# Seven instead of six seven-product pairs in the first row group, one instead of two new ones in the second

## The reference

```python
F = 5120                                       # x is (1024, 10240), W1 (256, 5120), fp32
x1, x2 = (x[:, :F], x[:, F:])
h1 = leaky_relu(layer_norm(x1 @ W1.T))         # layer_norm has no eps, no scale; leak 0.05
h2 = leaky_relu(layer_norm(x2 @ W1.T))
h1 = leaky_relu(layer_norm(h1 @ W2.T))         # W2 (64, 256)
h2 = leaky_relu(layer_norm(h2 @ W2.T))
h = jnp.concatenate([h1, h2], axis=-1)
h = leaky_relu(layer_norm(h @ W3.T))           # W3 (8, 128)
return h @ W4.T                                # W4 (1, 8)
```

## Time and profile before

| | us |
|---|---|
| median of 3 runs | 232.88 (232.81 to 232.94) |
| the profiled execution, its own time | 233.68 |
| its span in the profile | 231.9 |
| PE busy in the span | 224.6 (97%), 999 matmuls |
| DVE busy | 191.4 (83%) |
| ACT busy | 151.7 (65%) |
| POOL busy | 28.8 (12%) |
| DMA | 51.93 MB, mean 224 GB/s |

### The profile page before, as it was taken

How to read it: one execution, slowest core, us unless ns; L and a number is a source line. 1 busy time by engine, 2 the same in 40 slices (tenths; PEclk the granted TensorE clock), 3 DMA queues, 4 the chain that set the end, 5 groups by cost and what they waited for, 6 DMA issues and landing times.

```text
span 231.9 us, 2894 instructions
## 1 busy us (share of the span) xinstructions
PE 224.6 (97%) x999; PEld 179.3 (77%) x999; DVE 191.4 (83%) x245; ACT 151.7 (65%) x240; POOL 28.8 (12%) x41
## 2 busy tenths in 40 slices
PE   6999999999999999999999999999999999999992
PEld 2678786888887888888868888888888878888772
DVE  2689999978959999997669699999989699979324
ACT  3797989859588598963678453665546484824630
POOL 0000020020100200000012224427001400000014
PEclk9999999999999999999999999999999999999995
DMA  5999999999879999446839958668677414150000
GB/s 178 370 378 373 409 341 294 347 272 343 290 214 371 340 276 296 171 161 230 300 54 231 291 164 275 228 212 245 215 251 251 148 69 128 56 181 1 3 0 1
DMA packets 17950, 51.93 MB, mean 224 GB/s; under 512 B 2772, under 2 KB 3156, under 8 KB 17936
## 3 DMA queue, kind: packets, MB, share of 16 engines
q1 hardware_dynamic: 16064, 48.86, 60.5%
q0 software_dynamic: 1872, 2.89, 8.0%
HBM read 50.95 MB, written 0.01 MB: 220 GB/s over the span
## 4 chain that ended last, share of the span: by engine, by line
PE 82%; DMA 5%; DVE 4%; ACT 4%; issue 1%; POOL 1%; SPq 1%; POOLq 0%; DVEq 0%
PE acc L1004 79%; DMA xe_raw<-x 5%; PE acc L1126 2%; DVE xe_lo L703 2%; ACT xe_hi L588 2%; ACT unused L542 1%; DVE x_sum L758 1%; PE acc L1139 1%; ACT xt_hi L588 1%; DVE x_sum L768 1%; ACT we_hi L548 0%; POOL inv L485 0%; ACT stage L548 0%; PE acc L1147 0%; PE acc L1155 0%
## 5 line engine op out<-in xcount | busy, mean ns | idle before, releaser
L1004 PE MATMUL acc<-xe_lo,we_hi 128*128 128x512 f32 x176 | 68.8, 391 | 0.3 <-DVE xe_lo L703 0.2
L1004 PE MATMUL acc<-xe_hi,we_lo 128*128 128x512 f32 x176 | 68.5, 389 | 0.0
L703 DVE TENSOR_TENSOR xe_lo<-xe_raw,xe_hi 128x1024 fp32r<-128x1024 f32 (+1 forms) x48 | 55.6, 1177 | 15.2 <-ACT xe_hi L588 15.1
L588 ACT CAST xe_hi<-xe_raw 128x1024 fp32r<-128x1024 f32 (+1 forms) x48 | 47.9, 1009 | 30.7 <-PE acc L1004 22.1
L1004 PE MATMUL acc<-xe_hi,we_hi 128*128 128x512 f32 x176 | 48.3, 391 | 0.0
L1004 PEld LDWEIGHTS acc<-xe_lo,we_hi 128*128 128x128 f32 x176 | 33.0, 188 | 8.4 <-issue 1.7
L1004 PEld LDWEIGHTS acc<-xe_hi,we_hi 128*128 128x128 f32 x176 | 32.9, 188 | 7.4 <-issue 0.7
L1004 PEld LDWEIGHTS acc<-xe_hi,we_lo 128*128 128x128 f32 x176 | 33.1, 188 | 6.7
L588 ACT CAST xt_hi<-x_sum 128x2048 fp32r<-128x2048 f32 x14 | 26.7, 1910 | 12.8 <-DVE x_sum L774 12.8
L703 DVE TENSOR_TENSOR xt_lo<-x_sum,xt_hi 128x2048 fp32r<-128x2048 f32 x14 | 32.0, 2289 | 1.9 <-ACT xt_hi L588 1.9
L1004 PE MATMUL acc<-xt_lo,ws_hi 128*128 128x512 f32 x64 | 25.0, 391 | 0.1
(11 more groups left out here) (107 smaller groups left out, 274.4 us busy)
## 6 DMA issues: line engine op xcount, KB each, us to landing
xe_raw<-x SPq DMA_DIRECT2D x51, 512.0 KB, 5.5
xs_raw<-x SPq DMA_DIRECT2D x14, 768.0 KB, 5.8
stage<-w SPq DMA_DIRECT2D x21, 256.0 KB, 5.8
x_sum<-x SPq DMA_DIRECT2D x10, 256.0 KB, 3.4
x_sum<-x SPq DMA_DIRECT2D x4, 512.0 KB, 4.5
x_sum<-x POOLq DMA_DIRECT2D x4, 512.0 KB, 8.0
xe_raw<-x SPq DMA_DIRECT2D x2, 256.0 KB, 4.2
stage<-w SPq DMA_DIRECT2D x2, 128.0 KB, 3.3
```

The lines of the kernel that those rows point to most:

```text
L588: act.copy(hi_of(u, part), raw_of(u, part)).then_inc(hi_ready[part.buffer], 1)
L703: dve.tensor_tensor(lo_of(u, part), raw_of(u, part), hi_of(u, part).bitcast(F32), ALU.subtract)\
L1004: return pe.matmul(acc[:, bank, :], w, x, start=first, stop=True, skip_group_check=True)
```

## The change

The first group has seven instead of six S units and thirteen instead of fourteen E units; the S units with transfers that add are S2 to S6 (five) instead of S2 to S5 (four). In the second group the count of S units stays eight, but only one of them (pair 7) is new, instead of two (pairs 6 and 7). The first group's order goes from EHE SEE SEE SEE SE SE SEEL to EHE SEE SE SE SE SE SE SEEL. `centre_w23` follows S4 (unit 12), the same unit as before, when it was S3.

```diff
-SEVEN = 6
-MIXED = 2
+SEVEN = 7
+MIXED = 1
 BOTH = SEVEN + MIXED
...
-ORDER = ("EHE" + "SEE" * 3 + "SE" * 2 + "SEEL", "FE" + "SE" * 8 + "D")
+ORDER = ("EHESEE" + "SE" * 5 + "SEEL", "FE" + "SE" * 8 + "D")
...
-                if es[0].n == W23_UNIT + 3:
+                if es[0].n == W23_UNIT + 4:
                     centre_w23()
```

## The result

| | kernel before | changed kernel |
|---|---|---|
| first comparison, median | 232.91 us (232.81 to 233.38, 4 runs) | 235.08 us (233.85 to 236.16, 4 runs) |
| ratio, 95% interval | | 1.008 [1.0048, 1.0111] |
| second comparison, later, median | 233.26 us (35 runs) | 233.65 us (232.19 to 237.36, 12 runs) |
| ratio, 95% interval | | 1.0027 [0.9996, 1.0058] |

The changed kernel is slower by 0.8% in the first comparison. In the second it reads 0.3% slower, but the interval takes in 1, so no difference is shown there. I had forecast 232.04. The medians are over all runs; the ratios leave out runs more than 1.5% above the fastest of their kernel, one of the changed kernel's twelve (237.36) among them.

A forecast was written before the change was run, and what follows sets the result against it. PE was taken as the bound from 39 us on, feeders only needing to be early. Savings 0.68 + 0.16 = 0.84 us, so 232.88 - 0.84 = 232.04 us; range 231.9 to 233.8.

The forecast's parts named there:

- PE's saving of 0.68 us: Group 0, units 7 to 11: an S unit replaces an E unit, 3 matmuls less at 0.2267 us each.
- 0.16 us of the SEE: Two SEE of units 6 to 11 disappear with their late second E units; their 0.16 us counted as won.
- Group 1, "worth nothing": One new S unit less relieves DVE, ACT and SP, but PE's own 90.31 us hides it; no gain.
- DVE's ledger: Table for S2 to S6 of third-sum starts, weights' lo ends and PE's need times; leads of 1.25 to 2.31 us.
- The chain load, add, third sum: After lo of T: load, 4.77 us to the add's issue, its landing, then third sum two S units later.
- 56.93 + L: Landing time of S4's adding transfer, L being its latency; with 9.8, DVE waits 0.96 us and PE loses nothing.
- rival 2: Adding transfers eat the gain: S4's latency over 10.1, S5's third sum too late; 232.88, no change; chance 0.23.
- S4 alone late: Only S4's adding transfer is late; PE waits its latency minus 10.1 through S5's third sum.
- Rival 3: Slower: adding-transfer loop bounds at S5's third sum, costing twice the latency over 10.1; 233.85 at 11; chance 0.15.
- What would show it wrong: PE idle before S5's weights' lo near 82.4 after DVE waits for x_sum, or E-unit casts releasing PE.
- its figure of 358 GB/s: HBM-to-core rate making the SE period 11.0 us, longer than PE's; set aside for a 421 GB/s window.
- The Trainium skill's rule on GpSimd's descriptors: GpSimd-issued transfers wait during certain DVE two-port modes, so adds slowest where DVE is gapless; given no time.

The follow-up runs named there:

- small_later: Changed kernel with the W2/W3 centring moved to DVE's idle spot inside unit 20 and the small W2, W3, W4 loads eight units later; median 233.67 us, ratio 1.001.
- before_one_new: Kernel before with W1's sums of pair 6 left out in the second group, so one new S unit instead of two (probe only); median 232.80 us, ratio 0.9995.

## Why the prediction was wrong

- *PE's saving of 0.68 us, and 0.16 us of the SEE:* right; S1 to S4 took 30.60 us, and the stretch without adds agrees.
- *Group 1, "worth nothing":* wrong by 0.30 us. I read PE's unbroken 90.31 us as proof that nothing waits there. The chain merges matmuls over short gaps; a late weight load costs its time without a break in the row. The starts of the units would have shown it, as I had used them in group 0: in the kernel before, that period is 10.50 us instead of 10.20.
- *DVE's ledger:* DVE's pace was right to 0.01 us. Its latest times for PE were 0.22 us too late, since it took the matmul (0.68 us) where the weight load (0.46 us) waits: the latest third sum of S5 is 78.06, not 78.28, and that of S4 67.86, where 68.22 was measured.
- *The chain load, add, third sum:* this is the step that failed: "56.93 + L", "I take 9.8" and "No loss, but nearly". L for S4 was 10.0, nearly as taken. The load leg was the mis-sized term: I took 4.77 us (4.80 with the issue) from a place where no add was under way, and it was 6.0 for S4 and 6.6 for S5. Of the 1.49 us by which S4's third sum came later than forecast (68.22, not 66.73), 1.24 are this leg and 0.2 are L. With the leg and the weight load as measured, the L at which PE begins to wait at S5 is not 10.1 but about 8.6, which the 9.8 that I took is over. S3's add took 9.9 where I took 8.5; that cost DVE 0.77 us, but PE nothing. The rows for the load leg were there: 42.16 and 57.85 are loads issued while no add moves, and after the change the loads of two blocks for S4, S5 and S6 are issued into the previous unit's add. I had counted that adds come closer together and priced it in the mean load of the DMA engines (9.7 of 10.2 us), not in the latency of the one request that waits.
- *Rivals 2 and 3* named the place (S5's third sum) and the releaser (lo of the S weights). What both profiles of the changed kernel show is the case that rival 2 called "S4 alone late", with L at 10.0 and 9.9, at which its formula gives no wait. Rival 3's rule, that the L's of S3 and S5 add up, is not what held PE there; small_later's profile comes nearest to it, with 9.4 for S3 and 11.4 for S5. The range to 233.8 stopped at L = 11. Latencies seen at 7.5 to 9.8 us with a threshold that is in truth at 8.6 should have had a much larger chance and a longer tail.
- *The size:* the profile closes at -0.84 - 0.30 + 1.75 = +0.61 us in the stretch. The median of the first comparison was 2.17 us over the kernel before, so some 1.6 us of it are in no profile of the changed kernel. small_later's run of 235.19 shows how such a loss can come about; that the changed kernel's slower runs are like it is an inference.
- *What would show it wrong* came as listed: DVE waiting for x_sum, then PE's wait before lo of S5.
- *The Trainium skill's rules:* its figure of 358 GB/s (page "SBUF — State Buffer", section "A bandwidth-pool intuition that's wrong (but worth ruling out)") would have given the right sign. I had set it aside by one window at 421 GB/s. Over 45 to 85 us the changed kernel moved 282, 349, 285 and 315 GB/s in the four windows of 10 us at a DMA share of 0.95 to 1.07. The kernel before moved 278, 328, 289 and 299 at 0.92 to 1.03 in the same windows and PE lost nothing to DMA there, and the changed kernel's first three periods took 10.20 us each, not the 11.0 of that estimate. So the mean rate does not tell the two apart, and the page's cause is not shown. A peak window was still the wrong row for a queue that must be served in time.
- *The Trainium skill's rule on GpSimd's descriptors* (page "SBUF — State Buffer", section "SBUF: two separate sides"): it is about DVE in two-port modes, and I read it as one about DVE being busy. No run here shows which mode DVE's operations were in, and none was made to test the rule. Adds of 6.0 to 11.4 us occurred with DVE doing the same kinds of work, so how busy DVE was does not explain them. What does, beyond the small loads perhaps, stays open.

## What to carry to other kernels

When a change brings two transfers of one dependent chain closer together, price the chain with each leg's latency while the other is under way; the mean load of the DMA engines does not show it. Where the latency of a transfer scatters by more than the lead in hand, keep a spacing rather than a maximum of offloading: here three adding transfers, every other S unit, beat five, and were level with four. Take as the latest time of an operand the weight load that waits for it, not the matmul behind it. And check a bound of "PE only" by the starts of the units, not by an unbroken row of the chain.

## What I had not expected of the hardware

- From 40 us on, a load of two blocks (512 KB) took 3.5 to 5.0 us to land with no adding transfer under way, in 26 cases of 27; the other took 6.0 (before_one_new, at 41.24). Issued into the middle of one, as at S4 and S5 of the changed kernel and its variants, it took 5.4 to 6.7 us, and once, at S6 of small_later, 8.2. With 2.1 us or less of the adding transfer left to go it took 4.4 to 5.7 (five cases).
- S4's adding transfer took 9.7 to 10.0 us in the five profiles with three small loads (8 to 64 KB) issued within 3 us of it, and 7.2 to 8.5 us in the three without them. Other adds scattered from 6.0 to 11.4 us for reasons that no run separates.
- The start, up to the first S matmul of unit 6, ended at 40.07 to 41.69 us in the eleven profiles whose kernels do the same kinds of work up to there, and at 39.98 to 41.16 in the three without S2's adding transfer. That is as much as the whole effect of this change.
